# Masks of the first layer: GpSimd adds them to the bias in both halves of an answer, where TensorE added them by a product in the second

## The reference

```python
xn = layernorm(x, g_in)
q = (xn @ Wq).reshape(b, n, H, DH).transpose(0, 2, 1, 3) * scale   # 16 heads of 64
k, v = split(xn @ Wkv)                                             # one k and v for all heads, a null key and value ahead
sim = einsum('bhid,bjd->bhij', q, k) + bias                        # bias: 16 x 256 x 256, an input
sim = where(causal_mask, neg, sim)
sim = where(mask_p[:, None, None, :], sim, neg)                    # which keys of each sequence are valid
out = einsum('bhij,bjd->bhid', softmax(sim), v) @ Wo
return layernorm(out, g_out)
```

## Time and profile before

| | us |
|---|---|
| median of 3 runs | 416.53 (414.62 to 417.41) |
| the profiled execution's own time | 419.1 |
| its span, first to last instruction | 417.3 |
| busy: TensorE, VectorE, ScalarE, GpSimd | 351.6, 270.1, 242.2, 180.3 |
| GpSimd: masks to the bias of the first layer (L760, 32) | 23.8 |
| TensorE: products with the masks (L1192, 128) | 23.2 |
| granted TensorE clock, mean share of the full | 0.951 |

### The profile page before, as it was taken

How to read it: one execution, slowest core, us unless ns; L and a number is a source line. 1 busy time by engine, 2 the same in 40 slices (tenths; PEclk the granted TensorE clock), 3 DMA queues, 4 the chain that set the end, 5 groups by cost and what they waited for, 6 DMA issues and landing times.

```text
span 417.3 us, 7881 instructions
## 1 busy us (share of the span) xinstructions
PE 351.6 (84%) x2658; PEld 260.8 (62%) x2658; DVE 270.1 (65%) x945; ACT 242.2 (58%) x801; POOL 180.3 (43%) x258
## 2 busy tenths in 40 slices
PE   0459978898799898988899789978995989899896
PEld 0357766676667666665676566756674767578465
DVE  2755499979685667756558877767648335467562
ACT  2135576687488677767667868665864752132130
POOL 1334034537742776557456765585552142200000
PEclk9995899999899999998899999978997999999989
DMA  5840010232022961272020102020201100000000
GB/s 195 321 137 3 0 41 11 53 42 50 2 53 59 126 86 37 53 296 51 2 53 2 53 2 53 2 51 2 51 20 33 34 22 0 0 2 12 15 0 25
DMA packets 26640, 21.38 MB, mean 51 GB/s; under 512 B 2420, under 2 KB 25960, under 8 KB 26216
## 3 DMA queue, kind: packets, MB, share of 16 engines
q1 hardware_dynamic: 25608, 20.37, 19.7%
q10 hardware_dynamic: 992, 0.51, 0.9%
HBM read 19.84 MB, written 1.04 MB: 50 GB/s over the span
## 4 chain that ended last, share of the span: by engine, by line
PE 57%; DVE 19%; ACT 10%; POOL 7%; issue 5%; DMA 1%; ACTq 0%; DVEq 0%; POOLq 0%
PE bank L1215 8%; PE bank L1197 8%; PE bank L1206 6%; PE bank L1237 6%; DVE sb_prob L988 5%; ACT sb_prob L633 4%; ACT sb_pT L641 3%; PE bank L1192 3%; PE bank L1328 2%; PE bank L1324 2%; PE bank L1300 2%; PE bank L1157 2%; DVE sb_xn L907 2%; POOL sb_rq L741 2%; PE bank L1169 2%
## 5 line engine op out<-in xcount | busy, mean ns | idle before, releaser
L633 ACT ACTIVATE sb_prob<-sb_prob,sb_low 128x128 f32<-128x128 f32 (+1 forms) x256 | 113.5, 445 | 48.3 <-DVE sb_low L988 48.2
L641 ACT ACTIVATE sb_pT<-bank 128x512 f32<-128x512 f32 x96 | 56.0, 584 | 19.2 <-PE bank L1206 19.0
L1215 PE MATMUL bank<-sb_pT,sb_v_a 128*64 128x256 f32 x384 | 57.5, 406 | 10.0 <-ACT sb_pT L641 9.1
L1206 PE MATMUL bank<-sb_ident,sb_prob 128*128 128x128 f32 x384 | 60.8, 288 | 3.6 <-ACT sb_prob L633 1.9
L1206 PEld LDWEIGHTS bank<-sb_ident,sb_prob 128*128 128x128 f32 x384 | 43.1, 145 | 21.3 <-issue 16.0
L1197 PE MATMUL bank<-sb_kT,sb_qT_hi 64*128 64x256 f32 (+1 forms) x512 | 54.2, 296 | 1.5 <-DVE sb_low L988 0.9
L988 DVE CUSTOM_DVE_ANT_0 sb_prob<-bank,sb_nb,sb_t 128x128 f32<-128x128 f32 x128 | 38.6, 342 | 25.0 <-PE bank L1197 24.9
L633 ACT ACTIVATION_READ_ACCUMULATOR sb_prob<-sb_prob,sb_low 128x1 f32 x256 | 48.2, 188 | 0.0
L1197 PEld LDWEIGHTS bank<-sb_kT,sb_qT_hi 64*128 64x128 f32 x512 | 42.7, 201 | 8.2 <-issue 4.3
L988 DVE CUSTOM_DVE_ANT_0 sb_prob<-bank,sb_toep,sb_t 128x256 f32<-128x256 f32 x64 | 27.9, 474 | 27.5 <-PE bank L1197 27.5
L1215 PEld LDWEIGHTS bank<-sb_pT,sb_v_a 128*64 128x64 f32 x384 | 23.7, 139 | 25.7 <-issue 17.8
(11 more groups left out here) (184 smaller groups left out, 726.2 us busy)
## 6 DMA issues: line engine op xcount, KB each, us to landing
sb_r_rows<-recip_rows SPq DMA_DIRECT2D x30, 256.0 KB, 4.0
sb_packed<-in_packed SPq DMA_DIRECT2D x1, 2992.0 KB, 11.0
sb_bias<-in_bias SPq DMA_DIRECT2D x1, 2048.0 KB, 15.7
sb_toep<-bias_table SPq DMA_DIRECT2D x8, 256.0 KB, 12.7
sb_stage<-in_L_cond_Wq SPq DMA_DIRECT2D x2, 512.0 KB, 4.6
sb_bias<-in_bias SPq DMA_DIRECT2D x1, 1024.0 KB, 7.9
sb_wo<-in_L_cond_Wo SPq DMA_DIRECT2D x1, 512.0 KB, 13.8
sb_wo<-in_L_cond_Wout SPq DMA_DIRECT2D x1, 512.0 KB, 6.6
```

Of the source, the lines that this page charges most:

```text
L633: act.activation(p[:, j], p[:, j], ACT.Exp, scale=-1.0, bias=low[:, buf, half, h:h + 1], accum_out=total[:, buf, half, h:h + 1]).then_inc( ...
L641: act.activation(pT[:, c % PT_SLOTS].rearrange("p j q -> p (j q)"), t_ring.bank("T", s, n)[:], ACT.Copy).then_inc(t_ring.frees("T", s, n), 1)
L1206: ins = pe.transpose(dst[:, j * P:j * P + P], p[:, j % 2, kb * P:kb * P + P], ident[:])
L1215: ins = pe.matmul(dst[j * DH:j * DH + DH, 0:N], v_a[:, buf, kb], pT[:, c % PT_SLOTS].rearrange("p (i j) q -> p j i q", j=2)[:, j], start=( ...
```

## The change

`biased(s, i)` says for which steps GpSimd makes `nb`: all of the first layer, the first halves of the second. `cut` pieces are put in the list for these, in the first layer for the second half too and as far ahead (3.45 steps). `BIASED` lists them in their order, and slots, waits and `nb_made` go by the place in it. A slot of `nb` is 2 x 256 elements in place of 2 x 128, there are still 8. In a second half of the first layer `S` leaves out the mask products and its waits for the mask, and its first product now clears the bank; `min` reads `nb`. The second layer computes as before.

```diff
@@ -116,6 +116,11 @@
     return TRANSPOSED.index((g, kb))
 
 
+def biased(s, i):
+
+    return layer_of(s) == 0 or i < PAIRS
+
+
 def attention_order():
     items = []
 
@@ -153,7 +158,7 @@
                 put(base + sums, "q_sums", s, t)
                 put(base + norm, "q_norm", s, t)
         for i in range(STEPS):
-            if i < PAIRS:
+            if biased(s, i):
                 put(base + i - at["cut"], "cut", s, i)
             put(base + i + at["min"], "min", s, i)
             put(base + i + at["exp"], "exp", s, i)
@@ -234,6 +239,8 @@
 
 ORDER = attention_order()
 
+BIASED = [(s, i) for kind, s, i in ORDER if kind == "cut"]
+
 
 class Ring:
 
@@ -361,7 +368,7 @@
     mask = [mask_of_0, sb("mask1", [P, B, N], F32R)]
     even = sb("even", [P, P])
     even_r = sb("even_r", [P, P], F32R)
-    nb = sb("nb", [P, NB_SLOTS, 2, P])
+    nb = sb("nb", [P, NB_SLOTS, 2, N])
     minus_half = sb("minus_half", [P, H])
     stats = sb("stats", [P, 2, 6])
     mv = sb("mv", [P, 2, 2])
@@ -747,17 +754,20 @@
                 pool.tensor_tensor(t0[:, s % 2, n], t0[:, s % 2, n], null_bias[:, 1], ALU.subtract)\
                     .then_inc(t0_made, 1)
             if kind == "cut":
-                c = PAIRS * s + n
+                c = BIASED.index((s, n))
+                half, pair = divmod(n, PAIRS)
+                keys = P * (half + 1)
                 w.wait_ge(masks_made, lay + 1)
                 if lay == 0:
-                    w.wait_ge(bias_cut, 1)
+                    w.wait_ge(bias_cut, half + 1)
                 else:
                     w.wait_ge(toep_loaded, 16 * (P // ROWS))
                 if c >= NB_SLOTS:
-                    of, i = divmod(c - NB_SLOTS, PAIRS)
+                    of, i = BIASED[c - NB_SLOTS]
                     w.wait_ge(masked, 2 * (STEPS * of + i) + 2)
-                tile = bias0[:, 2 * n:2 * n + 2] if lay == 0 else toep[:, 2 * n:2 * n + 2, P:N]
-                pool.tensor_tensor(nb[:, c % NB_SLOTS], mask[lay][:, b:b + 1, 0:P].bitcast(F32).to_broadcast([P, 2, P]),
+                tile = (bias0, bias1)[half][:, 2 * pair:2 * pair + 2] if lay == 0 else toep[:, 2 * n:2 * n + 2, P:N]
+                pool.tensor_tensor(nb[:, c % NB_SLOTS, :, 0:keys],
+                                   mask[lay][:, b:b + 1, 0:keys].bitcast(F32).to_broadcast([P, 2, keys]),
                                    tile, ALU.add).then_inc(nb_made, 1)
             if kind == "scale" and n < 2:
                 for g in range(4 * n, 4 * n + 4):
@@ -972,19 +982,14 @@
                 if c >= PROB_SLOTS:
                     of, i = divmod(c - PROB_SLOTS, STEPS)
                     w.wait_ge(*t_ring.filled("T", of, tile_of(i // 2, i // PAIRS)))
-                if half == 0:
-                    w.wait_ge(nb_made, PAIRS * s + n + 1)
-                elif lay == 0:
-                    w.wait_ge(bias_cut, 2)
+                if biased(s, n):
+                    w.wait_ge(nb_made, BIASED.index((s, n)) + 1)
                 else:
                     w.wait_ge(toep_loaded, 16 * (P // ROWS))
                 w.wait_ge(s_done, c // 2 + 1)
                 for j in range(2):
                     h = 2 * pair + j
-                    if half == 0:
-                        bias = nb[:, (PAIRS * s + n) % NB_SLOTS, j]
-                    else:
-                        bias = (bias1 if lay == 0 else toep)[:, h]
+                    bias = nb[:, BIASED.index((s, n)) % NB_SLOTS, j, 0:keys] if biased(s, n) else toep[:, h]
                     ins = dve.tensor_tensor_reduce(p[:, j], s_bank[j][:, n % 2 * keys:n % 2 * keys + keys],
                                                    bias, -1.0, t0[:, buf, half, h:h + 1],
                                                    ALU.add, ALU.min, low[:, buf, half, h:h + 1])
@@ -1181,12 +1186,13 @@
                     w.wait_ge(masked, 4 * c)
                 w.wait_ge(*t_ring.emptied("kt", s, half))
                 w.wait_ge(*q_emptied(s, half, 2 * g + 1))
-                if half == 1:
+                whole = not biased(s, 2 * n)
+                if whole:
                     w.wait_ge(even_made, 1)
                     w.wait_ge(masks_made, lay + 1)
                 keys = P * (half + 1)
                 for i in range(2):
-                    if half == 1:
+                    if whole:
                         for j in range(2):
                             rows = slice(j * DH, j * DH + DH)
                             pe.matmul(s_bank[j][:, i * keys:i * keys + keys], even_r[rows], mask[lay][rows, s % B],
@@ -1196,7 +1202,7 @@
                             rows = slice(j * DH, j * DH + DH)
                             ins = pe.matmul(s_bank[j][:, i * keys:i * keys + keys],
                                             lhs[rows, buf, 2 * g + i, half * P:half * P + P],
-                                            kT[rows, buf, part, 0:keys], start=(half == 0 and k == 0), stop=(k == 2))
+                                            kT[rows, buf, part, 0:keys], start=(not whole and k == 0), stop=(k == 2))
                 ins.then_inc(s_done, 1)
             if kind == "T":
                 g, kb = TRANSPOSED[n]
```

## The result

The change makes the kernel slower. Four timed runs of it took 422.66 to 426.70 us, median 426.0; those of the kernel before, on the same chip, 414.62 to 420.55, median 416.97. The ratio is 1.0193 with a 95% interval of 1.0102 to 1.0285. In a second series it was 1.0193 again (1.0129 to 1.0257). I had forecast 420.1 us and no more than 423.5.

A forecast was written before the change was run, and what follows sets the result against it. TensorE, busy 84% of the span and working in fixed order, was taken as the bound. First to fourth answer and clock, 0.3 + 0.5 - 0.9 + 2.4 + 1.3 = +3.6 us, on 416.53 gave 420.1 us; range 413.0 to 423.5.

The forecast's parts named there:

- Additions of 1.25 us, 40 us of GpSimd: First layer: 32 added additions of 512 columns at 1.25 us each, 40 us more GpSimd work.
- Fourth answer, +2.4: First layer's fourth answer: additions delay total, VectorE's reciprocal and TensorE's transpose Z (+3.0); net +2.4 us after savings.
- The stop before Z: Fourth answer: TensorE stands still about 3.3 us before the transpose Z, waiting for shares.
- Second answer, the late total and addition 14, +0.5: Second answer: total +1.2 us late, up to +1.1 from VectorE's tensor_scalar operations waiting on addition 14; net +0.5 us.
- Third answer, the late total is covered: Third answer: total's delay is covered by 0.2 us before the next S; three batches' saving arrives, -0.9 us.
- The saving, 0.31 us a batch: Sixteen first-layer S batches on TensorE each lose four mask products, saving 0.31 us (bounds 0.24, 0.34); gross 5.0 us.
- What they delay is what stands behind them on GpSimd: No minimum waits for its own bias; the additions delay only later GpSimd work, such as below and total.
- the pair at 56.62: First answer: two tensor_scalar operations on VectorE meet additions of 1.25 us, +0.3 to +1.0, taken as 0.6 us.
- Clock, +1.3 from one fall behind the stop before Z: Fourth answer: TensorE's granted clock falls once after its stop before Z, +1.3 us (bounds nothing and 3.4).
- the first (the late total is worth nothing): Rival: Z of the fourth answer is not late, so savings come through, 411.5 or 413.4 us; no stall, chance 0.18.
- The second (longer falls of the clock, 423.9 us): Rival: clock low past some 4 us behind Z, +3.4 for +1.3, and slower additions; 423.9 us, chance 0.15.
- The third (the stall without the clock): Rival: the fourth answer's stall comes but the clock does not fall; 418.8 us, chance 0.22.

The follow-up runs named there:

- runs 3: The changed kernel with the change kept in the fourth answer alone, the first three answers as before; ratio to the kernel before 1.0110.
- 6: The changed kernel with the additions of steps 12 and 13 moved behind total and shares; ratio to the kernel before 1.0298.
- 7: The changed kernel with the additions of steps 12 and 13 behind total and shares, and ten nb slots for eight; ratio to the kernel before 1.0076.

## Why the prediction was wrong

The sign of the mechanism was right and most of the fourth answer's working; the sum was too small by more than half (3.6 us; the timed medians differ by 9.0).

- *Additions of 1.25 us, 40 us of GpSimd*: right.
- *Fourth answer, +2.4*: right, measured +2.3 in the whole change and alone. The stop before Z (I wrote 3.3 us) was 2.8 where the clock did not fall ahead of it.
- *Second answer, the late total and addition 14, +0.5*: nearly, +0.7.
- *Third answer, the late total is covered*: right; the saving was 0.6, not 0.9.
- *The saving, 0.31 us a batch*: too much. It is 0.23 to 0.25 where it arrives, my lower end of 0.24, and it arrives for about nine batches: 2.2 us of the 5.0 that I called gross. My terms held some 2.1 us of savings in the end, so this moved the sum by little; but it sets what any version could win.
- *"What they delay is what stands behind them on GpSimd"*: **this is the first step that failed.** I charged what is behind the additions on GpSimd's own queue, and of what VectorE has beside them two places only: the pair at 56.62 (+0.6; with the product behind it, it is +1.27) and the tensor_scalar operations beside addition 14. I did not go through VectorE's timeline for every other operation between SBUF tiles that would now meet an addition. There were two: the product L1049 in the second answer (+0.83) and the `tensor_scalar` L823 in the third (+0.77). In the trace of before both lie in stretches where GpSimd stands idle (it waits for the minima, from 79.84 to 84.19 and from 116.9 to 121.5), which is just where the additions of steps 8 to 10 go. That is 2.3 us missing. I had read those stretches as free. By itself it would put the sum at 422.4 us, still within my range; it is this and the clock's term together that put the time outside.
- *Clock, +1.3 from one fall behind the stop before Z*: **the second step that failed.** In four of five profiles the fall came ahead of the stop and was hidden in it, so it cost nothing; in the third it came behind Z, as I had said, and cost 1.5. What the clock took besides, in the mean of the five, was +3.3 us behind the mark, in the second layer, which I had not considered at all, and in the first layer some 0.8 in all. Why it falls more there with the change stays open.
- *Rivals*: the first (the late total is worth nothing) is refuted by runs 3, 6 and 7. The second (longer falls of the clock, 423.9 us) comes nearest in time, but its condition, a clock still low 4 us behind Z, was met in one profile of five (the third, by a single stretch that ended 4.7 us behind Z), so the nearness is luck. The third (the stall without the clock) has the fourth answer right in the other four, +2.3, and the whole time wrong.

The ledger in us, change less before, means of five profiles: up to step 7 of the first answer -0.8 (the starts differ, nothing is changed there), and at step 8 its one saving, -0.2; from there to the mark +6.1, of which the steps above make 5.3 and low stretches of the clock most of the rest; from the mark to the end +3.3. Together +8.4, and the timed medians differ by 9.0. Against my +3.6: the locked operations 2.3 more, the other steps of the answers 0.5 more, the clock 2.8 more (4.1 for 1.3), the start 0.8 less.

I had used the rule in the Trainium skill, "SBUF — State Buffer", section "Who interferes with whom", only for `tensor_scalar`. The section also says that an operation of VectorE with two SBUF inputs contends with a GpSimd instruction that reads SBUF, and that one with at most one SBUF input outside the two-port modes, and a reduction on this chip, do not. The trace agrees in each of these: the product with two SBUF inputs 1.24 for 0.42, the subtraction with one in PSUM 0.68 for 0.68, the reduction 1.20 for 1.20.

## What to carry to other kernels

An engine's idle time is not free when another engine shares something with it: before moving work to GpSimd, go through VectorE's timeline in each stretch where the work will run, mark every `tensor_scalar` and every operation with two SBUF operands, and charge each with up to the length of one GpSimd instruction; cut the instructions short, or place them beside reductions and operations on PSUM. Measure early what the removal alone is worth: here it was 2.2 us, half a per cent of the kernel's time, and a ratio that could not be told from no change even with nothing put in its place. And where a ring of slots is given out in one engine's order, moving a piece moves the slot of each piece behind it.

## What the runs showed of the hardware that I had not expected

- A `tensor_scalar` of sixteen columns (0.24 us alone) took 1.00 us beside a GpSimd addition, and 0.74 beside additions of half the length: the wait is for one instruction, however small one's own is.
- It goes the other way too. VectorE's subtraction L949 (two SBUF operands) ran from 119.69 for 0.50 us when GpSimd reached its next addition at 119.87; that one took 1.46 us, thirty of the 32 between 1.26 and 1.31. VectorE was first, and GpSimd waited. The only other long one, 1.45 us from 83.42, stands beside L1054, which had its turn between the second addition and this third one:

```profile
119.69 0.50 DVE L949 TENSOR_TENSOR sb_k_src<-sb_kn,sb_k_src 128x256 fp32r<-128x256 f32 x1
...
119.87 1.46 POOL L769 TENSOR_TENSOR sb_nb<-sb_mask,sb_bias 128x512 f32<-128x512 f32 x1
```
- The granted clock's low stretches fall in nearly the same places in repeated profiles of one kernel (202, 222 and 242 us in four of five with the change, 217 and 237 in three of five before it). With the change they lie elsewhere. What they cost depends on whether they meet a wait: nothing ahead of the stop in the fourth answer, 1.5 us just behind it, some 3 us in the second layer.
